# Self-attention over eight images on one core: row maxima brought to their row by small copies instead of TensorE turns

## The chip, the core and the metric

The kernel runs on one core of a Trainium2 chip. A core has TensorE (PE in the profile; its weight loads are shown apart as PEld), VectorE (DVE), ScalarE (ACT), GpSimd (POOL) and SyncE (SP), each with its own instruction stream; they meet only at semaphores. Here SP only issues copies (DMAs), which 16 DMA engines carry out. The metric is the device time of one execution in microseconds; of several executions the median is taken. The profile describes one execution.

## What is computed

For each of 8 images with 128 channels and 32x32 = 1024 pixels, a 1x1-convolution attention block:

```python
xf = x.reshape(b, c, n)                       # n = 1024
q = einsum('oc,bcn->bon', Wq, xf) + bq        # 64 channels
k = einsum('oc,bcn->bon', Wk, xf) + bk        # 64 channels
v = einsum('oc,bcn->bon', Wv, xf) + bv        # 128 channels
attn = softmax(einsum('bci,bcj->bij', q, k), axis=-1)
out = einsum('bcn,bmn->bcm', v, attn)
return gamma * out + x
```

All of it is float32. The kernel splits operands into a rounded high part (fp32r) and a rest, so that fast matmuls keep the accuracy.

## The kernel before, in words

**Steps.** The work is cut into 8 images x 2 halves x 8 tiles = 128 steps. Step s belongs to image b = s // 16 and to place k = s % 16 in it. A half (512 query pixels) is called a chunk; chunk c = 2b + h has the steps 8c to 8c + 7. At step s TensorE does, in this order: the scores of step s + 2 (`score_tile`, two matmuls of 512 columns, L510 and L511), one or two matmuls for row maxima of a later chunk (`do_max`, L468), the weighted sums of step s - 2 (`sums_hi`, four matmuls of 258 columns, L529; after every fourth step also `sums_lo`, 16 matmuls, L545), and then the side jobs of that place in the image: the projections `qk` (L455 to L457) and `v` (L462) of a coming image, the turning of a finished output chunk `out` (L478), and `mt`.

**The row maxima.** The softmax needs the maximum of each query's scores before its exponentials. For a chunk, eight matmuls (L468, two for each of its four query tiles) give scores in PSUM; DVE reduces each to `neg_max` (L740), and `round_max` (L747) makes of them `neg_max_r`, 128 partitions x 4 columns: queries lie across the partitions. The scores matmul L511 wants them along one row instead, `q_lomax[64, chunk]`, which the row of ones in `k_hione` adds to every score. Before the change the job `mt` does this: four turns on TensorE against `identity_r` (L473, `turn_max`) into a PSUM bank, and an ACT copy of one row of 512 (L660, `write_max_rows`), which raises `max_rows_done`. `mt` stands at the end of step k = 4 (for the second chunk of the same image) and of k = 12 (for the first chunk of the next).

**Two banks.** `work` has two PSUM banks. The jobs mx (a maximum's matmul), qk, v, mt and out take them in turn, in the order `WORK_ORDER`; each waits until the job two places ahead of it has been read out. After a `qk` job, for instance, the second job behind it waits until ACT has written `qk_hi` (L643) and DVE `qk_lo` (L731) from that bank.

**Copies between partitions.** `spread(n)` on SP sends q and k of image n to the partitions where the matmuls want them: six copies of 256 KB, four of which (semaphore `spread_mx`) the first maximum matmul of image n waits for, and two (`spread_rest`) its first scores. It waits until image n - 2 has no scores left to do, since the buffers alternate; `spread(b + 2)` thus starts at place k = 13 of image b. `store_y` stores an output chunk, `load_x` loads an image. SP does all of these in a fixed order.

**Exponentials.** ACT makes two exponentials a step from a scores bank (L676 and L679); the scores of step s + 2 wait for the second of step s, since there are two scores banks.

## Time and profile before

| | us |
|---|---|
| median of 3 runs | 248.56 (247.63 to 250.33) |
| the profiled execution, its own time | 247.75 |
| the profiled execution, its span | 246.0 |
| PE busy | 233.6 (95%) |
| ACT busy | 189.0 (77%) |
| POOL busy | 176.5 (72%) |
| DVE busy | 170.7 (69%) |

The span runs from the first to the last instruction; 1.75 us of the execution's time lie around it. A matmul's busy time is its own stretch from start to modelled end, and matmuls overlap, so for TensorE the distance from one start to the next says what an instruction costs; the starts in the rows below are read for that. TensorE's clock stood at full speed over the whole span (0.997 on average).

### The profile page before, as it was taken

The page shows a single profiled execution, that of the slowest core. Times are in us where ns is not written, and L with a number is a line of the kernel's source. Part 1 is how long each engine was busy: PE and PEld are TensorE (multiplying, and loading weights), DVE is VectorE, ACT ScalarE, POOL GpSimd, SP SyncE. Part 2 cuts the span into 40 slices and gives each one's busy share as a digit, 9 for nine tenths or more (in the row PEclk, how much of TensorE's full clock was granted, in tenths as well). Part 3 has the DMA queues.
Part 4 walks back from the last instruction along what each step waited for, and adds up shares of the span by engine and source line. Part 5 has one row for each costly group of instructions (what it writes and reads, how often), then busy time and mean ns, then how long its engine had stood idle before and what let it go on. Part 6 is the DMA issues. An engine that isn't in the chain of part 4 may idle for free.

```text
span 246.0 us, 4933 instructions
## 1 busy us (share of the span) xinstructions
PE 233.6 (95%) x1738; PEld 200.3 (81%) x1738; DVE 170.7 (69%) x287; ACT 189.0 (77%) x359; POOL 176.5 (72%) x158
## 2 busy tenths in 40 slices
PE   7998988999999999999999999999999999999992
PEld 7365867888879898898879888898888889898891
DVE  1667295876888767776878767877768767784354
ACT  2868956788787888779877887788877878879841
POOL 8578986299963897469962898558982877668760
PEclk9999999999999999999999999999999999999998
DMA  4706400570409312390407504191105601010102
GB/s 97 237 29 145 113 0 4 128 173 3 128 0 223 79 45 87 85 217 0 131 0 174 129 0 129 34 229 40 45 0 124 177 3 45 0 45 0 44 15 73
DMA packets 8040, 19.85 MB, mean 81 GB/s; under 512 B 1744, under 2 KB 2256, under 8 KB 8016
## 3 DMA queue, kind: packets, MB, share of 16 engines
q1 hardware_dynamic: 7776, 19.50, 30.3%
q8 instruction: 14, 0.23, 0.4%
q14 instruction: 10, 0.08, 0.1%
q10 hardware_dynamic: 240, 0.03, 0.1%
HBM read 4.33 MB, written 4.19 MB: 35 GB/s over the span
## 4 chain that ended last, share of the span: by engine, by line
PE 88%; ACT 5%; DVE 5%; issue 1%; POOL 0%; POOLq 0%; DVEq 0%; ACTq 0%
PE sums L529 24%; PE sums L545 12%; PE scores L510 12%; PE work L468 11%; PE scores L511 11%; PE work L462 5%; PE work L478 3%; DVE qk_lo L731 2%; ACT qk_hi L643 2%; PE work L473 2%; PE sums L559 2%; PE work L457 1%; PE work L456 1%; PE work L455 1%; DVE neg_max L740 1%
## 5 line engine op out<-in xcount | busy, mean ns | idle before, releaser
L392 POOL TENSOR_TENSOR weight_lo<-weight,weight_hi 128x512 bf16<-128x512 f32 x90 | 124.5, 1402 | 48.6 <-ACT weight_hi L679 48.2
L740 DVE TENSOR_REDUCE neg_max<-work 128x1 f32<-128x512 f32 x120 | 81.7, 686 | 25.5 <-PE work L468 25.3
L676 ACT ACTIVATE weight<-scores 128x512 f32<-128x512 f32 x128 | 76.6, 599 | 22.6 <-PE scores L511 18.9
L529 PEld LDWEIGHTS sums<-values,weight_hi 128*128 128x128 f32 x512 | 78.1, 188 | 9.9 <-issue 0.5
L529 PE MATMUL sums<-values,weight_hi 128*128 128x258 f32 x512 | 81.7, 282 | 0.1
L679 ACT ACTIVATE weight_hi<-scores 128x512 fp32r<-128x512 f32 x128 | 76.5, 597 | 0.0
L510 PE MATMUL scores<-q_hihi,k_hilo 128*128 128x512 f32 x128 | 55.1, 430 | 1.2 <-ACT weight_hi L679 1.1
L511 PE MATMUL scores<-q_lomax,k_hione 128*128 128x512 f32 x128 | 50.4, 394 | 0.0
L468 PE MATMUL work<-k_hilo,q_hihi 128*128 128x512 f32 x120 | 48.6, 411 | 1.7 <-DVE qk_lo L731 0.9
L779 DVE TENSOR_TENSOR weight_lo<-weight,weight_hi 128x512 bf16<-128x512 f32 x38 | 35.7, 940 | 2.4 <-ACT weight_hi L679 2.4
L545 PE MATMUL sums<-values_b,weight_lo 128*128 128x130 bf16 x512 | 35.5, 221 | 0.0
L468 PEld LDWEIGHTS work<-k_hilo,q_hihi 128*128 128x128 f32 x120 | 22.5, 187 | 13.7 <-DVE values L736 3.8
L545 PEld LDWEIGHTS sums<-values_b,weight_lo 128*128 128x128 bf16 x512 | 29.8, 98 | 1.6
L510 PEld LDWEIGHTS scores<-q_hihi,k_hilo 128*128 128x128 f32 x128 | 24.2, 189 | 2.9 <-ACT weight_hi L679 1.9
L511 PEld LDWEIGHTS scores<-q_lomax,k_hione 128*128 128x128 f32 x128 | 24.3, 190 | 0.6
L787 DVE TENSOR_TENSOR total<-sums,low_sum 128x258 f32<-128x258 f32 x32 | 13.6, 427 | 13.9 <-ACT low_sum L685 13.3
L685 ACT ACTIVATE low_sum<-sums 128x256 f32<-128x256 f32 x32 | 12.4, 387 | 7.2 <-PE sums L545 5.1
L399 POOL TENSOR_TENSOR scaled<-total,one_over 128x512 f32<-128x512 f32 x15 | 15.6, 1042 | 0.0
L462 PE MATMUL work<-w_v_t,x_sb 128*128 128x128 f32 x112 | 15.5, 281 | 0.0
L373 POOL TENSOR_TENSOR x_lo<-x_sb,x_hi 128x512 fp32r<-128x512 f32 x12 | 15.5, 1288 | 0.0
L384 POOL TENSOR_SCALAR values_b<-values 128x512 bf16<-128x512 f32 x16 | 9.9, 620 | 7.6 <-ACT values L654 7.6
L736 DVE TENSOR_TENSOR values<-work,values 128x512 fp32r<-128x512 f32 x14 | 9.7, 692 | 7.3 <-ACT values L654 7.3
(78 smaller groups left out, 186.4 us busy)
## 6 DMA issues: line engine op xcount, KB each, us to landing
out<-y_sb SPq DMA_DIRECT2D x15, 256.0 KB, 2.5
x_sb<-in_x SPq DMA_DIRECT2D x7, 512.0 KB, 4.4
q_hihi<-qk_hi SPq DMA_DIRECT2D x14, 256.0 KB, 4.4
k_hilo<-qk_hi SPq DMA_DIRECT2D x7, 256.0 KB, 3.1
k_hilo<-qk_lo SPq DMA_DIRECT2D x7, 256.0 KB, 5.1
q_lomax<-qk_lo SPq DMA_DIRECT2D x7, 256.0 KB, 5.2
k_hione<-qk_hi SPq DMA_DIRECT2D x7, 256.0 KB, 5.1
x_sb<-in_x SPq DMA_DIRECT2D x2, 256.0 KB, 3.5
```

The source lines that it names most:

```text
L392: pool.tensor_tensor(weight_lo[:, r], weight[:, r], weight_hi[:, r], ALU.subtract).then_inc(weight_lo_pool_done, 1)
L399: pool.tensor_tensor(scaled[:, :], total[:, :, 0:CHANNELS], by, ALU.mult).then_inc(scaled_done, 1)
L462: last = pe.matmul(place[:, tile(t)], image(n)[:, tile(half * CHUNK_TILES + t)], w_v_t[:, :], start=True, stop=True)
L468: pe.matmul(place, q_hihi[p][:, tile(t)], k_hilo[p][:, chunk(h)], start=True, stop=True).then_inc(mx_done, 1)
L510: pe.matmul(scores[:, s % 2], k_hilo[p][:, tile(j)], q_hihi[p][:, chunk(h)], start=True, stop=False)
L511: pe.matmul(scores[:, s % 2], k_hione[p][:, tile(j)], q_lomax[p][:, chunk(h)], start=False, stop=True).then_inc(scores_done, 1)
L529: last = pe.matmul(sums[:, it, 0:VCOLS], weight_hi[:, r, tile(it)], values[p][:, j], start=(j == 0), stop=False)
L545: return pe.matmul(sums[:, it, CHANNELS:VCOLS], weight_lo[:, i % RING, tile(it)], values_b[p][:, j], start=False, stop=(j == TILES - 1))
L676: act.activation(weight[:, r], scores[:, s % 2], ACT.Exp)
L679: act.activation(weight_hi[:, r], scores[:, s % 2], ACT.Exp).then_inc(weight_hi_done, 1)
L740: dve.reduce_max(neg_max[:, h, t:t + 1], place, AX.X, negate=True).then_inc(neg_max_done, 1)
L779: dve.tensor_tensor(weight_lo[:, r], weight[:, r], weight_hi[:, r], ALU.subtract).then_inc(weight_lo_done, 1)
```

## The change

The job `mt` is gone except for chunks 0 and 1. For the chunks 2 to 15 SP sends the maxima itself: `send_max_row` issues four copies, each of one column of `neg_max_r` (128 partitions x 4 bytes) into 128 elements of the row of `q_lomax`. The scores of such a chunk wait for `max_row_sent` and no longer for `max_rows_done`. The maxima of a chunk are found two steps earlier (chunk c in steps 8c - 14 to 8c - 7, before 8c - 12 to 8c - 5). Two maxima of chunk 1 move ahead of the first step, the place of six idle turns (`keep_busy`) there is taken by the second projection of image 1, whose `qk_lo` moves on DVE behind the maxima of step 0. The maxima of image 1 (chunks 2 and 3) follow a table over steps 5 to 17. `neg_max` is laid out with its two halves side by side, and `round_max` is a reduction over them.

```diff
-WARM_UP = (14, 4, 6)
+WARM_UP = (14, 4)
...
+EARLY = 18
+EARLY_MAXES = {5: (2, 0, 1), 6: (2, 1, 2), 7: (2, 3, 1), 8: (2, 4, 2), 9: (2, 6, 1), 10: (2, 7, 1),
...
 def max_jobs(s):
-    if s < 4:
-        return [(1, 2 * s), (1, 2 * s + 1)]
-    if s < 12:
-        return [(2, 2 * (s - 7)), (2, 2 * (s - 7) + 1)] if 7 <= s < 11 else []
-    chunk = (s + 12) // TILES
-    return [(chunk, (s + 12) % TILES)] if chunk < CHUNKS else []
+    if s < 3:
+        return [(1, 2 * s + 2), (1, 2 * s + 3)]
+    if s < EARLY:
+        c, first, count = EARLY_MAXES.get(s, (0, 0, 0))
+        return [(c, i) for i in range(first, first + count)]
+    chunk = (s + 14) // TILES
+    return [(chunk, (s + 14) % TILES)] if chunk < CHUNKS else []
...
-    if k == 4:
-        jobs.append(("mt", 2 * b + 1, 0))
+    if b == 0 and k == 4:
+        jobs.append(("mt", 1, 0))
...
-    if k == 12 and b + 1 < BATCHES:
-        jobs.append(("mt", 2 * b + 2, 0))
...
+FIRST_MAXES = [("mx", 1, 0), ("mx", 1, 1)]
+WORK_ORDER = FIRST_MAXES + [job for s in range(ALL_STEPS)
+                            for job in [("mx", c, i) for c, i in max_jobs(s)] + side_jobs(s)]
...
+        def wait_max_row(engine, c):
+            if c < HALVES:
+                engine.wait_ge(max_rows_done, c + 1)
+            else:
+                engine.wait_ge(max_row_sent[c % 2], 16 * CHUNK_TILES * (c // 2))
...
+            def send_max_row(c):
+                n, h = divmod(c, HALVES)
+                sp.wait_ge(neg_max_r_done, c + 1)
+
+                wait(sp, scores_done, STEPS * (n - 2) + TILES * (h + 1))
+                for t in range(CHUNK_TILES):
+                    at = h * CHUNK_TILES + t
+                    row = q_lomax[n % 2][HEAD:HEAD + 1, tile(at)].bitcast(fp32)
+                    sp.dma_start(row.rearrange("a (i b) -> a i b", b=1),
+                                 neg_max_r[:, at:at + 1].bitcast(fp32)).then_inc(max_row_sent[c % 2], 16)
...
             for b in range(BATCHES):
                 if b > 0:
+                    send_max_row(2 * b + 1)
                     store_y(2 * b - 1)
                     if b + IMAGES - 1 < BATCHES:
                         load_x(b + IMAGES - 1)
+                if b + 1 < BATCHES:
+                    send_max_row(2 * b + 2)
                 if b + 2 < BATCHES:
                     spread(b + 2)
                 store_y(2 * b)
...
                 if j == 0:
-                    pe.wait_ge(max_rows_done, HALVES * b + h + 1)
+                    wait_max_row(pe, HALVES * b + h)
...
-            for h in range(HALVES):
-                pe.wait_ge(neg_max_done, CHUNK_TILES + h + 1)
-                project_qk(1, h, sums[:, h])
+            pe.wait_ge(first_hi_done, len(FIRST))
+            for name, c, i in FIRST_MAXES:
+                do_max(c, i)
+            pe.wait_ge(neg_max_done, CHUNK_TILES + 1)
+            project_qk(1, 0, sums[:, 0])
             pe.wait_ge(neg_max_r_done, 1)
             pe.wait_ge(pool_setup, SETUP_MADE)
             turn_max(0, sums[:, 2])
-            keep_busy(WARM_UP[2], sums[:, 3])
+            project_qk(1, 1, sums[:, 1])
...
-                wait(dve, mt_done, c - 1)
-                dve.tensor_tensor(neg_max_r[:, cols], neg_max[:, 0, cols], neg_max[:, 1, cols],
-                                  ALU.min).then_inc(neg_max_r_done, 1)
+                if c < 2 * HALVES:
+                    wait(dve, mt_done, c - 1)
+                else:
+                    wait_max_row(dve, c - HALVES)
+                dve.tensor_reduce(neg_max_r[:, cols], neg_max[:, cols], AX.X, ALU.min).then_inc(neg_max_r_done, 1)
...
-            for h in range(HALVES):
-                rest_of_qk(1, h, sums[:, h])
+            for name, c, i in FIRST_MAXES:
+                do_max(c, i)
+            rest_of_qk(1, 0, sums[:, 0])
...
+                if s == 0:
+                    rest_of_qk(1, 1, sums[:, 1])
```

The order on TensorE before, from the second `qk` job (k = 11) of an image in the middle to the maximum of k = 13; lines are those of the kernel before:

```order
L455 MATMUL work<-x_hi,w_qk_hi 128x512
L456 MATMUL work<-x_hi,w_qk_lo 128x512
L457 MATMUL work<-x_lo,w_qk_hi 128x512
L510 MATMUL scores<-q_hihi1,k_hilo1 128x512
L511 MATMUL scores<-q_lomax1,k_hione1 128x512
L468 MATMUL work<-k_hilo0,q_hihi0 128x512
L529 MATMUL sums<-values1,weight_hi 128x258 x4
L473 MATMUL work<-identity_r,neg_max_r 1x128 x4
L510 MATMUL scores<-q_hihi1,k_hilo1 128x512
L511 MATMUL scores<-q_lomax1,k_hione1 128x512
L468 MATMUL work<-k_hilo0,q_hihi0 128x512
```

The same piece of the changed kernel, with its own line numbers (the `qk` job is L482 to L484, scores L537 and L538, a maximum L495, sums L556):

```order
L482 MATMUL work<-x_hi,w_qk_hi 128x512
L483 MATMUL work<-x_hi,w_qk_lo 128x512
L484 MATMUL work<-x_lo,w_qk_hi 128x512
L537 MATMUL scores<-q_hihi1,k_hilo1 128x512
L538 MATMUL scores<-q_lomax1,k_hione1 128x512
L495 MATMUL work<-k_hilo0,q_hihi0 128x512
L556 MATMUL sums<-values1,weight_hi 128x258 x4
L537 MATMUL scores<-q_hihi1,k_hilo1 128x512
L538 MATMUL scores<-q_lomax1,k_hione1 128x512
L495 MATMUL work<-k_hilo0,q_hihi0 128x512
```

The four turns are gone; the job that stands second behind `qk`, and so waits for its `qk_lo`, is now the last row, a maximum's matmul one pair of scores later.

The order on SP before, over one image, from one `spread` to the next:

```order
L302 DMA k_hilo<-qk_lo 64x1024 [waits qk_lo_done]
L303 DMA q_lomax<-qk_lo 64x1024
L304 DMA k_hione<-qk_hi 64x1024
L308 DMA out<-y_sb 128x512 [waits y_done] x2
L291 DMA x_sb<-in_x 128x1024
L298 DMA k_hilo<-qk_hi 64x1024 [waits scores_done,qk_hi_done]
```

And in the changed kernel (L327 is a copy of one column of maxima, L332 a store, L304 the load of an image, L311 the first copy of the next `spread`):

```order
L315 DMA k_hilo<-qk_lo 64x1024 [waits qk_lo_done]
L316 DMA q_lomax<-qk_lo 64x1024
L317 DMA k_hione<-qk_hi 64x1024
L332 DMA out<-y_sb 128x512 [waits y_done]
L327 DMA q_lomax<-neg_max_r 1x128x1 [waits scores_done,neg_max_r_done]
L327 DMA q_lomax<-neg_max_r 1x128x1 x3
L332 DMA out<-y_sb 128x512 [waits y_done]
L304 DMA x_sb<-in_x 128x1024
L327 DMA q_lomax<-neg_max_r 1x128x1 [waits scores_done,neg_max_r_done]
L327 DMA q_lomax<-neg_max_r 1x128x1 x3
L311 DMA k_hilo<-qk_hi 64x1024 [waits scores_done,qk_hi_done]
```

Two groups of four small copies stand between the large ones: one between the two stores, one ahead of the next `spread`.

## Rows read from the trace of the kernel before

**Rows 1.** The page, part 1: busy time and share of the span

```profile
PE 233.6 (95%) x1738; PEld 200.3 (81%) x1738; DVE 170.7 (69%) x287; ACT 189.0 (77%) x359; POOL 176.5 (72%) x158
```

**Rows 2.** Waits: who waited for whom; us in total, times, longest

```profile
PE work L473 <- DVE qk_lo L731: 2.4, 6, 0.4
...
PE scores L510 <- ACT weight_hi L679: 1.1, 2, 0.7
```

**Rows 3.** Timeline of PE, image 2, k = 12 and 13: start, us, instruction

```profile
99.26 0.64 PE L529 MATMUL sums<-values,weight_hi 128*128 128x258 f32 x4
100.28 0.40 PE L473 MATMUL work<-identity_r,neg_max_r 128*1 128x128 f32 x4 [0.39 <-DVE qk_lo L731]
100.52 0.44 PE L510 MATMUL scores<-q_hihi,k_hilo 128*128 128x512 f32 x1
100.80 0.40 PE L511 MATMUL scores<-q_lomax,k_hione 128*128 128x512 f32 x1
```

**Rows 4.** Timeline of PE, image 3, k = 2 to 5

```profile
110.51 0.64 PE L529 MATMUL sums<-values,weight_hi 128*128 128x258 f32 x4
110.99 0.40 PE L510 MATMUL scores<-q_hihi,k_hilo 128*128 128x512 f32 x1
111.22 0.40 PE L511 MATMUL scores<-q_lomax,k_hione 128*128 128x512 f32 x1
...
112.92 0.64 PE L529 MATMUL sums<-values,weight_hi 128*128 128x258 f32 x4
113.39 0.40 PE L473 MATMUL work<-identity_r,neg_max_r 128*1 128x128 f32 x4
113.63 0.44 PE L510 MATMUL scores<-q_hihi,k_hilo 128*128 128x512 f32 x1
113.91 0.40 PE L511 MATMUL scores<-q_lomax,k_hione 128*128 128x512 f32 x1
```

**Rows 5.** Busy time by stretch, one image from spread to spread

```profile
core 0: us, PE busy (x) PEld busy (x) DVE busy (x) ACT busy (x) POOL busy (x), PEclk, DMA share, GB/s
101.28:129.62 28.34, 27.94 (x216) 24.43 (x214) 21.43 (x36) 23.13 (x45) 21.04 (x18) 1.00 0.36 94
```

**Rows 6.** Timeline of DVE: qk_lo of k = 11, last maximum of k = 1

```profile
99.48 0.75 DVE L731 SCALAR_TENSOR_TENSOR qk_lo<-work,b_qk,qk_hi 128x512 fp32r<-128x512 f32 x1 [0.84 <-ACT qk_hi L643]
...
107.64 0.69 DVE L740 TENSOR_REDUCE neg_max<-work 128x1 f32<-128x512 f32 x1 [0.23 <-PE work L468]
```

**Rows 7.** Timeline of PE, early steps: waits at k = 8, 10 and 12 of image 0

```profile
33.80 0.50 PE L468 MATMUL work<-k_hilo,q_hihi 128*128 128x512 f32 x1 [0.87 <-DVE qk_lo L731]
...
39.49 0.50 PE L468 MATMUL work<-k_hilo,q_hihi 128*128 128x512 f32 x1 [0.71 <-DVE values L736]
...
43.68 0.40 PE L473 MATMUL work<-identity_r,neg_max_r 128*1 128x128 f32 x4 [0.40 <-DVE qk_lo L731]
```

**Rows 8.** Timeline of SP: start and length of the issue of each copy

```profile
4.67 0.43 SPq L317 DMA_DIRECT2D b_v<-in_L_conv_bv  x1
...
21.58 1.15 SPq L302 DMA_DIRECT2D k_hilo<-qk_lo  x1
...
101.28 0.47 SPq L298 DMA_DIRECT2D k_hilo<-qk_hi  x1
...
103.10 1.14 SPq L302 DMA_DIRECT2D k_hilo<-qk_lo  x1
```

**Rows 9.** Timeline of PE: maximum of k = 2, scores at k = 6, image 3

```profile
110.28 0.39 PE L468 MATMUL work<-k_hilo,q_hihi 128*128 128x512 f32 x1
...
115.81 0.48 PE L510 MATMUL scores<-q_hihi,k_hilo 128*128 128x512 f32 x1
```

**Rows 10.** DMA view of 100 to 112 us: engines busy by 0.3 us, us to landing

```profile
DMA  0000000099995999998999989999999987200000
...
k_hilo<-qk_lo SPq DMA_DIRECT2D x1, 256.0 KB, 4.9
...
out<-y_sb SPq DMA_DIRECT2D x1, 256.0 KB, 4.8
```

**Rows 11.** The page, part 6: a copy of 128 elements of 4 bytes

```profile
b_v<-in_L_conv_bv SPq DMA_DIRECT2D x1, 0.5 KB, 2.6
```

More of the change, by code:

```diff
@@ L42 @@
 SPREAD_MX, SPREAD_REST = 4, 2
+EARLY = 18
+EARLY_MAXES = {5: (2, 0, 1), 6: (2, 1, 2), 7: (2, 3, 1), 8: (2, 4, 2), 9: (2, 6, 1), 10: (2, 7, 1),
+               11: (3, 0, 1), 12: (3, 1, 2), 13: (3, 3, 1), 14: (3, 4, 1), 15: (3, 5, 1), 16: (3, 6, 1), 17: (3, 7, 1)}
 def max_jobs(s):
-    if s < 4:
-        return [(1, 2 * s), (1, 2 * s + 1)]
-    if s < 12:
-        return [(2, 2 * (s - 7)), (2, 2 * (s - 7) + 1)] if 7 <= s < 11 else []
-    chunk = (s + 12) // TILES
-    return [(chunk, (s + 12) % TILES)] if chunk < CHUNKS else []
+    if s < 3:
[5 more added lines that the diff above has]
+    return [(chunk, (s + 14) % TILES)] if chunk < CHUNKS else []
 def side_jobs(s):
@@ L73, in side_jobs @@
     return jobs
-WORK_ORDER = [job for s in range(ALL_STEPS)
-              for job in [("mx", c, i) for c, i in max_jobs(s)] + side_jobs(s)]
+FIRST_MAXES = [("mx", 1, 0), ("mx", 1, 1)]
+WORK_ORDER = FIRST_MAXES + [job for s in range(ALL_STEPS)
+                            for job in [("mx", c, i) for c, i in max_jobs(s)] + side_jobs(s)]
 PLACE = {job: n for n, job in enumerate(WORK_ORDER)}
@@ L168, in attention_program @@
         values_b = [sbuf(f"values_b{p}", [TILE, TILES, CHANNELS + 2], bf16) for p in range(2)]
-        neg_max = sbuf("neg_max", [TILE, 2, TILES], fp32)
+        neg_max = sbuf("neg_max", [TILE, TILES, 2], fp32)
         neg_max_r = sbuf("neg_max_r", [TILE, TILES], fp32r)
@@ L227, in attention_program @@
         max_rows_done = sem("max_rows_done")
+        max_row_sent = [sem(f"max_row_sent{p}") for p in range(2)]
         w_ready = sem("w_ready")
@@ L597, in _ @@
             turn_max(0, sums[:, 2])
-            keep_busy(WARM_UP[2], sums[:, 3])
+            project_qk(1, 1, sums[:, 1])
             pe.wait_ge(first_q_lo_done, HALVES)
-            pe.wait_ge(first_hi_done, len(FIRST))
             for s in range(AHEAD):
@@ L739, in maximum @@
             def maximum(t, h, place):
-                dve.reduce_max(neg_max[:, h, t:t + 1], place, AX.X, negate=True).then_inc(neg_max_done, 1)
+                dve.reduce_max(neg_max[:, t, h:h + 1], place, AX.X, negate=True).then_inc(neg_max_done, 1)
             def round_max(c):
```

## The prediction

> **What bounds the kernel now.** I began with the busy times [rows 1]: PE has 95% of the span, ACT 77%, POOL 72%, DVE 69%. A busy PE says little, as its matmuls overlap, so I read PE's timeline by starts. Between spread and spread lies one image, 28.34 us [rows 5]; in it nothing but PE comes near (ACT 23.1, DVE 21.4, POOL 21.0). The reader should see there that matmuls follow each other at fixed distances: a 512-column matmul 0.23 us after the one before, a group of four sums 0.48 us [rows 4], with hardly any waiting. The table of waits confirms it: after the first microseconds TensorE waits for little but banks, and the largest single item that belongs to the part that changes is the turn of the maxima behind `qk_lo`, 2.4 us in 6 waits [rows 2]. So PE's instruction stream is the path, and what leaves it counts in full, as long as nothing new is late.
>
> **A set of turns.** At k = 4 the set starts at 113.39 and the scores behind it at 113.63, 0.24 us; the second scores matmul then comes after 0.28 instead of 0.23; the sums ahead take 0.47 instead of 0.48 [rows 4]. One set costs 0.28 to 0.29 us. Fifteen sets run within the steps and 14 go. The Trainium skill, page "TensorE: Matmul & The Clock Gate", section on PE-mode transpose, gives about 275 ns for one 128x128 transpose in a kernel's context; by that figure a set would be 1.1 us and 14 sets 15.4 us, an estimate. The starts here contradict it: four turns in 0.24 us.
>
> **The wait ahead of k = 12's set.** From the sums at 99.26 to the turns at 100.28 are 1.02 us, where 0.48 would do: 0.54 us waiting for the bank of `qk`, which DVE's `qk_lo` of 99.48 to 100.23 gives back [rows 3, 6]. With the set gone, the second job behind `qk` is the maximum of k = 13. It comes after two scores matmuls: 99.26 + 0.48 + 2 x 0.23 = 100.20, against 100.28 when the bank is free. A matmul that had to wait also delays its successor by about 0.1 (its busy time reads 0.50 instead of 0.40 [rows 7, 9]). So some 0.18 of the 0.54 stays and 0.36 goes. Images 1 to 5 have this: 5 x 0.36 = 1.8 us. From below, the same wait could come back in full at the new place (0); from above it could all go (2.7).
>
> **The early steps (image 0).** Gone: a set (0.29); the wait for `values` at k = 10, since one maximum and not two stands behind `v` there (0.71 + about 0.2 of its train) [rows 7]; a short wait ahead of the first `qk`, about 0.3. Added: two maxima more before step 18 (0.46). The second maximum of k = 12 now waits for `qk_lo` ahead of the sums, so that this wait grows by about the 0.5 that the sums used to cover. The `qk_lo` of image 1 moves behind two maxima on DVE, by about 0.9 us, and SP's fourth copy of `spread(1)`, at 21.58 before, waits for it [rows 8]: with 4.9 us to landing [rows 10] it lands near 27.3, while the first maximum of chunk 2 now stands at step 5, near 26.9. That is a wait of about 0.5 us, and DVE's longer chain over steps 0 to 2 adds 0.4. Of these two, some 0.5 is taken up by the wait of 0.87 us at k = 8 [rows 7]. Gains 1.5, costs 1.9, absorbed 0.5: about +0.2 us net, and I would believe anything from -1 to +1.2. In the prologue, two maxima and one projection take the place of two projections, and the other projection that of the idle turns: about equal.
>
> **The end.** The two maxima that were moved early leave the last image: 2 x 0.23 = 0.46 us off. ACT has room there for one step more without a maximum.
>
> **The new wait.** It must be asked what is queued behind each new thing. On SP, the group for the second chunk of an image stands behind `store_y(2b)`, that for the first chunk of the next image behind `store_y` and `load_x`, both ahead of their deadlines. The tight one is the second chunk: its last maximum is now that of k = 1, reduced by 108.33, rounded by about 108.5 [rows 6]. No row shows such a copy between partitions. The nearest is b_v, also 128 elements of 4 bytes: issued in 0.43 us, landed after 2.6 [rows 8, 11]. Four of these: the last is issued near 109.9. The DMA engines are still full with `spread` and the store until about 110.5 [rows 10], so I let it land at 112.6 to 113.1. The scores of k = 6 that need it start at 115.81, or 115.5 without the set of k = 4 [rows 9]. That leaves over 2 us, and I cost the copies at nothing; their cover is these four steps of TensorE's own work. The far bound is the 256 KB copy of `qk_lo`, 1.15 us an issue and 4.9 to landing [rows 8, 10]: 108.5 + 3 x 1.15 + 4.9 = 116.9, 1.4 us too late. The first chunks have about 4 us to spare.
>
> The maxima also need their `spread` two steps earlier, at k = 2 instead of 4. The fourth copy is issued at 103.10 and lands 4.9 us later, at 108.0; the maximum of k = 2 stands at 110.28 [rows 8 to 10]. Two microseconds remain, or 1.1 if the 4.9 counts from the end of the issue. The small copies ahead of `spread` on SP go out some 5 us before it starts.
>
> DVE's reduction instead of a minimum of 128x4, and ACT's 14 row copies less, lie beside the path: nothing.
>
> **The sum.** 13 sets outside image 0 x 0.29 = 3.8; wait 1.8; image 0 +0.2; end 0.46. Together 6.2 us. Against the profiled execution's own 247.75 us this is 241.5; the median of the runs shown is 0.8 above that execution and gives 242.4. I say 242.0. By the bounds above the gain is 3.2 (early steps at -1, the wait returning) to 8.1 (early +1.2, the wait all gone), so this case spans 239.7 to 245.3, and I expect it mostly within 240.5 to 243.5.
>
> **Rivals.**
> *The copies are late (slower).* If four copies with 4-byte elements behave like the large ones, the scores of k = 6 wait 1.4 us in each of the six images 1 to 6 (image 7 has no `spread` ahead of it), and the first chunks, due near 130.1 and landing near 122.5 + 3 x 1.15 + 4.9 = 130.9, 0.8 us in each of seven: 8.4 + 5.6 = 14 us lost against 6.2 gained, 247.75 + 7.8 = 255.6. It decides from 116.5 us on, that is from 8 us between the rounded maximum and the last landing, where I expect 4.5. For it: each element is one small write to a single partition, and the DMA engines are full when the copies are issued. Against it: the b_v row. Chance 0.07. Two sections of the Trainium skill's page "DMA: Bandwidth & Descriptors" bear on it and point in opposite directions. Specifications: under 512 B a write is a read-modify-write, which speaks against the change. On the semaphore's 16: a copy is spread over up to 16 engines by the size of the slowest dimension of both sides, here 128 and 128, so each engine gets 8 elements and not one engine all 128. No row of this case shows either.
>
> *PE runs into the others' latencies.* Jobs closer together meet banks that are not yet free: the waits for `qk_lo` and `values` of 0.87 and 0.71 us [rows 7] in image 0 show what tight spacing costs. Half a microsecond in each of six images takes 3 us back: 245 (244.5 to 245.5). Against it: in the middle images such waits are under 0.1 us, and at most one job's order changes. The same price holds where rows land half a microsecond late. Chance 0.15.
>
> *Nothing changes.* The early steps lose 1 us, the wait returns in full at k = 13, and the copies are late by half a microsecond in every image: 6.2 - 1.2 - 1.8 - 3 = 0.2, about 248. For the path to stay where it is three small things must coincide. Chance 0.06.
>
> *More than the sum.* If turns cost TensorE more than their starts show, for instance by stalls that I cannot separate, 239.5. Chance 0.07. By the skill's 275 ns it would be near 232; I give that under 0.01, as the starts exclude it.
>
> The forecast keeps 0.65. Within 1% (2.5 us of 248.56, about what a measurement of this kernel can tell from no change) means 246.1 to 251.0. Faster holds the forecast, the larger gain and nearly all of the 245 case: 0.86. Same holds the last rival and a little of the 245 case: 0.07. Slower: 0.07. The range of 8 in 10 runs from 240.2 to 246.0; it leaves out the slower case, no change and part of the larger gain.
>
> **What would show it.** In the profile after: 8 turns of maxima and not 64; an image of 27.4 us instead of 28.34, spread to spread; a wait of TensorE for `qk_lo` at the maximum of k = 13 of under 0.2 us; no wait of the scores for a copy; small copies on SP of about 0.45 us each, landing in under 3.5 us; near step 5 a wait of TensorE of about 0.5 us behind the fourth copy of `spread(1)`. I am wrong if TensorE is idle at k = 6 or k = 2 of the middle images behind a DMA, or if the period stays above 28 us.

## The result

| | before | after |
|---|---|---|
| median of 4 runs each, us | 248.09 (247.48 to 250.33) | 241.16 (240.90 to 241.74) |
| ratio, 95% interval | | 0.9708 (0.9642 to 0.9773) |
| profiled execution / its span, us | 247.75 / 246.0 | 241.74 / 239.7 |
| PE, ACT, POOL, DVE busy, us | 233.6, 189.0, 176.5, 170.7 | 229.3, 179.6, 174.6, 169.5 |

The change makes the kernel 3% faster. The same kernel run again later, as the partner of the experiments, took 240.44 us (240.29 to 241.56, 6 runs) against 248.64, ratio 0.9681 (0.9651 to 0.9712). The forecast was 242.0, with a range of 240.2 to 246.0.

The page of the changed kernel, parts 1 and 6, answers to [rows 1]:

```profile
PE 229.3 (96%) x1676; PEld 196.8 (82%) x1676; DVE 169.5 (71%) x287; ACT 179.6 (75%) x345; POOL 174.6 (73%) x158
...
q_lomax<-neg_max_r SPq DMA_DIRECT2D x56, 0.5 KB, 2.1
```

PE is still the path. The last row is new: 56 small copies (14 chunks of four), landing a median 2.1 us after their issue.

One image from spread to spread, the view of [rows 5]:

```profile
98.91:126.23 27.32, 27.32 (x207) 23.95 (x208) 21.42 (x36) 21.81 (x43) 20.78 (x17) 1.00 0.40 98
```

An image takes 27.32 us instead of 28.34. The clock is at its full level in both, and ACT has two row copies less.

TensorE in image 2, k = 12 and 13, the place of [rows 3] (timeline: start, us, instruction):

```profile
97.72 0.64 PE L556 MATMUL sums<-values,weight_hi 128*128 128x258 f32 x4
98.20 0.39 PE L537 MATMUL scores<-q_hihi,k_hilo 128*128 128x512 f32 x1
98.43 0.40 PE L538 MATMUL scores<-q_lomax,k_hione 128*128 128x512 f32 x1
98.76 0.50 PE L495 MATMUL work<-k_hilo,q_hihi 128*128 128x512 f32 x1
99.11 0.64 PE L556 MATMUL sums<-values,weight_hi 128*128 128x258 f32 x4
```

Where 1.02 us lay between the sums and the turns, the scores now start 0.48 after the sums. What is left of the wait for the bank of `qk` stands ahead of the maximum of k = 13: it starts 0.33 after L538 instead of 0.23, and the sums 0.35 after it instead of 0.24 (0.24 as in the rows of k = 2 below, 108.10 to 108.33), together 0.2 us.

TensorE in image 3, the maximum of k = 2 and the scores of k = 6, the places of [rows 9]:

```profile
107.86 0.40 PE L538 MATMUL scores<-q_lomax,k_hione 128*128 128x512 f32 x1
108.10 0.39 PE L495 MATMUL work<-k_hilo,q_hihi 128*128 128x512 f32 x1
108.33 0.64 PE L556 MATMUL sums<-values,weight_hi 128*128 128x258 f32 x4
...
112.35 1.11 PE L572 MATMUL sums<-values_b,weight_lo 128*128 128x130 bf16 x16
113.27 0.48 PE L537 MATMUL scores<-q_hihi,k_hilo 128*128 128x512 f32 x1
```

Neither has a wait in brackets. The two stations of SP and DVE behind them are these (SP: issue; DVE: last maximum of k = 1 and its rounding):

```profile
100.76 1.17 SPq L315 DMA_DIRECT2D k_hilo<-qk_lo  x1
...
106.37 2.44 SPq L327 DMA_DIRECT2D q_lomax<-neg_max_r  x4
```

```profile
105.46 0.69 DVE L768 TENSOR_REDUCE neg_max<-work 128x1 f32<-128x512 f32 x1 [0.23 <-PE work L495]
106.18 0.16 DVE L778 TENSOR_REDUCE neg_max_r<-neg_max 128x4 fp32r<-128x8 f32 x1
```

The maxima are rounded at 106.34, the four copies are issued from 106.37 to 108.81, and the scores that need them start at 113.27, 4.5 us behind the end of the last issue. In the DMA view of 98.9 to 112 us the engines (one digit for 0.33 us) are full up to about 107.8 and at two tenths or less from 108.1 on, so the copies get through behind the store without trouble:

```profile
DMA  0007999599989999978999998994222020000000
```

**Where the 6.3 us of span went.** I cut both traces at the same instructions: the first scores (17.31 before, 17.79 after) and the first copy of `spread` (L298 before, L311 after) of images 2 and 7 (44.69 and 186.20 before, 44.54 and 180.84 after).

| stretch | before | after | gain |
|---|---|---|---|
| start to first scores | 17.31 | 17.79 | -0.48 |
| to `spread(2)` | 27.38 | 26.75 | 0.63 |
| five images, to `spread(7)` | 141.51 | 136.30 | 5.21 |
| to the end of the span | 59.8 | 58.9 | 0.9 |

The loss in the first stretch is not the change's. The first projection of that execution takes 1.88 us for two matmuls, where before the change it takes 1.02:

```profile
5.64 1.88 PE L598 MATMUL scores<-x_sb,w_kk_t 128*128 128x512 f32 x2
```

Its input was not late, for it starts at 5.64 as it did before (5.63); its matmuls are slow. They lie 0.86 us apart (5.64, 6.50, 7.35) where they lay 0.43 apart (5.63, 6.06, 6.49). The granted clock reads 1.00 in both, so the cause stays open. The profiles of experiments 8 and 9 show the same, others a part of it.

In the profile of the changed kernel's second set of runs it takes 1.02, the first scores start at 16.79, and the four stretches gain 0.52, 0.65, 5.13 and 1.2, together 7.5 (span 238.5). From the first projection to the first scores are 11.68 us before and 11.27 there, so the rewritten prologue is worth 0.4.

### The profile page after: what moved, and what is told of

Same layout as the page of the kernel before. It is cut to its first block, busy times and chain, and to the rows that moved or that the text cites. A ratio compares the mean times of both kernels' runs of the same rounds, so it can differ in the third digit from the quotient of the medians.

```text
span 239.7 us, 4848 instructions
## 1 busy us (share of the span) xinstructions
PE 229.3 (96%) x1676; PEld 196.8 (82%) x1676; DVE 169.5 (71%) x287; ACT 179.6 (75%) x345; POOL 174.6 (73%) x158
## 4 chain that ended last, share of the span: by engine, by line
PE 92%; DVE 3%; ACT 3%; issue 1%; POOL 0%; POOLq 0%; DVEq 0%
PE sums L556 25%; PE sums L572 13%; PE scores L537 12%; PE work L495 12%; PE scores L538 12%; PE work L489 6%; PE work L505 3%; PE sums L586 2%; PE work L483 1%; PE work L484 1%; PE work L482 1%; DVE neg_max L768 1%; DVE qk_lo L759 1%; PE scores L489 1%; PE sums L478 1%
## 5 line engine op out<-in xcount | busy, mean ns | idle before, releaser
L419 POOL TENSOR_TENSOR weight_lo<-weight,weight_hi 128x512 bf16<-128x512 f32 x90 | 122.5, 1381 | 43.6 <-ACT weight_hi L707 43.4
L556 PEld LDWEIGHTS sums<-values,weight_hi 128*128 128x128 f32 x512 | 78.1, 188 | 10.2 <-issue 0.5
L556 PE MATMUL sums<-values,weight_hi 128*128 128x258 f32 x512 | 81.7, 282 | 0.1
L537 PE MATMUL scores<-q_hihi,k_hilo 128*128 128x512 f32 x128 | 54.5, 426 | 1.1 <-ACT weight_hi L707 1.1
L495 PE MATMUL work<-k_hilo,q_hihi 128*128 128x512 f32 x120 | 48.9, 413 | 2.4 <-DVE qk_lo L759 2.0
L538 PE MATMUL scores<-q_lomax,k_hione 128*128 128x512 f32 x128 | 50.4, 393 | 0.0
L809 DVE TENSOR_TENSOR weight_lo<-weight,weight_hi 128x512 bf16<-128x512 f32 x38 | 36.5, 961 | 2.7 <-ACT weight_hi L707 2.7
L495 PEld LDWEIGHTS work<-k_hilo,q_hihi 128*128 128x128 f32 x120 | 22.4, 188 | 14.5 <-DVE qk_lo L759 6.5
L537 PEld LDWEIGHTS scores<-q_hihi,k_hilo 128*128 128x128 f32 x128 | 24.2, 189 | 3.2 <-ACT weight_hi L707 1.9
L538 PEld LDWEIGHTS scores<-q_lomax,k_hione 128*128 128x128 f32 x128 | 24.3, 190 | 0.6
```

Of the source, the lines that this page charges most:

```text
L419: pool.tensor_tensor(weight_lo[:, r], weight[:, r], weight_hi[:, r], ALU.subtract).then_inc(weight_lo_pool_done, 1)
L495: pe.matmul(place, q_hihi[p][:, tile(t)], k_hilo[p][:, chunk(h)], start=True, stop=True).then_inc(mx_done, 1)
L537: pe.matmul(scores[:, s % 2], k_hilo[p][:, tile(j)], q_hihi[p][:, chunk(h)], start=True, stop=False)
L538: pe.matmul(scores[:, s % 2], k_hione[p][:, tile(j)], q_lomax[p][:, chunk(h)], start=False, stop=True).then_inc(scores_done, 1)
L556: last = pe.matmul(sums[:, it, 0:VCOLS], weight_hi[:, r, tile(it)], values[p][:, j], start=(j == 0), stop=False)
L809: dve.tensor_tensor(weight_lo[:, r], weight[:, r], weight_hi[:, r], ALU.subtract).then_inc(weight_lo_done, 1)
```

## The experiments

All are the changed kernel with one edit; the kernel before ran beside them (median 248.61 to 248.65). A difference of two of these kernels is taken against 240.44, the changed kernel's second result. The reading to be tested: the turns' time on TensorE comes back in full, and the copies cost nothing as long as they land in time. Against it stood: the gain is due to ACT's missing copies or to the new order of the maxima; the copies cost something by themselves; and they land so close to the need that little would make them late.

**1. The turns alone put back** (`e1_turns_back`), same maxima, same copies: turns of columns of `identity_r` into the bank, at the old places and in the old order of banks, with nothing done with the result.

```diff
-    if b == 0 and k == 4:
+    if k == 4:
...
+    if k == 12 and b + 1 < BATCHES:
+        jobs.append(("mt", 2 * b + 2, 0))
...
+                elif name == "mt":
+                    for t in range(CHUNK_TILES):
+                        pe.transpose(place[0:1, tile(t)].bitcast(fp32r), identity_r[:, t:t + 1], identity_r[:, :])
```

> The changed kernel with the turns alone put back: at k = 4 and k = 12 TensorE again does four turns into a bank (of columns of the identity, their result is read by nobody; the maxima still travel by copies), and the jobs stand in the bank order of before. No ACT row copies. Theory A (TensorE's instruction stream is the path, and what left it is the gain): 14 sets at 0.35 us, the difference of k = 4 and 5 between the two traces, give 4.9 us, and the wait for qk_lo comes back ahead of the set of k = 12 in five images, about 0.33 each, 1.7: 241.2 + 6.6 = 247.8, between 247 and 248.5. Rival B (ACT's 14 row copies, or the chain from maxima to scores, were the cost): stays within 1 us of 241.2.

Measured: 246.70 us (245.78 to 247.55, 7 runs), ratio 0.9917 (0.9883 to 0.9951): a little below the band. An image takes 28.26 us again, and the wait is back at its old place:

```profile
99.75 0.64 PE L561 MATMUL sums<-values,weight_hi 128*128 128x258 f32 x4
100.79 0.40 PE L529 MATMUL work<-identity_r 128*1 128x128 f32 x4 [0.40 <-DVE qk_lo L764]
101.03 0.44 PE L542 MATMUL scores<-q_hihi,k_hilo 128*128 128x512 f32 x1
```

By the medians, 6.3 of the 8.2 us of the change come back with the turns and the wait in front of them. The middle of the two traces shows it most cleanly: the five images from `spread(2)` to `spread(7)` take 141.20 us here (45.34 to 186.54), 141.51 before the change and 136.38 in the changed kernel's second profile, so 4.8 of 5.1 us are back, 0.96 an image. Outside these images it isn't a pure price of the turns: in image 0 the extra set at k = 12 also shifts which bank the maxima there get, and one of them, at 34.81, waits 2.35 us for `qk_lo` where the changed kernel waits 1.16. By the medians it stays 1.9 us below the kernel before; of what it keeps of the change, prologue, order of the maxima and end, no run shows the shares. The two profiled executions are only 0.2 us apart (247.55 and 247.75), so the size of this rest is uncertain too.

**2. ACT's 14 copies put back** (`e2_act_copies_back`), into a spare row, in the old places.

```diff
...
+                if (k == 4 and b > 0) or (k == 12 and b + 1 < BATCHES):
+                    act.activation(spare_row[HEAD:HEAD + 1, :], k_hione[0][HEAD:HEAD + 1, chunk(0)], ACT.Copy)
```

> The changed kernel with 14 ACT copies of one row of 512 put back at the places of before (k = 4 and k = 12), between two places in SBUF that nobody else uses; no turns. Theory A: ACT has idle time at both places, no change, 240.8 to 241.8. Rival B (ACT's 0.59 us a copy was on the path): up to 14 x 0.59 = 8.2 us more, 249.

Measured: 240.95 us (240.24 to 241.07, 4 runs), ratio 0.9685 (0.9648 to 0.9722). ACT is busy 189.8 us instead of 179.6, and the time doesn't move. ACT's work left out was off the path.

**3. The maxima as late as before** (`e3_maxima_late`): copies, but the old schedule.

```diff
...
-    chunk = (s + 14) // TILES
-    return [(chunk, (s + 14) % TILES)] if chunk < CHUNKS else []
+    chunk = (s + 12) // TILES
+    return [(chunk, (s + 12) % TILES)] if chunk < CHUNKS else []
...
-FIRST_MAXES = [("mx", 1, 0), ("mx", 1, 1)]
+FIRST_MAXES = []
```

> The changed kernel with the maxima where they were before (chunk c in steps 8c - 12 to 8c - 5, the first steps by the old list, no maxima ahead of step 0), rows still sent by copies. By the trace of the changed kernel: the last maximum of a second chunk (k = 3) would be rounded near 110.6 instead of 106.3, the fourth copy issued 1.85 us later lands 2.2 to 2.3 us after that, at 114.7, and the scores of k = 6 want it at 113.3: 1.4 us late, seven times; first chunks land near 128.3 against 127.8, 0.5 late, seven times. Theory A with a copy's latency of about 4.1 us from the rounded maxima to the last landing: 241.2 + 9.8 + 3.5 + 0.5 for the first steps = 255, between 251 and 257. Rival (the copies are quick enough, and moving the maxima was not needed): 241 to 242.5.

Measured: 256.65 us (254.52 to 258.35, 4 runs), ratio 1.0293 (1.0218 to 1.0369), inside the band. The table of waits names the cause (us in total, times, longest):

```profile
PEld scores L536 <- DMA q_lomax<-neg_max_r: 14.2, 13, 2.1
...
PE scores L536 <- DMA q_lomax<-neg_max_r: 11.4, 10, 2.0
```

In image 3 the copies are issued from 113.99 (SP) and the scores start at 117.90 (PE), so from the first issue to usable scores are 3.9 us:

```profile
116.61 0.22 PE L571 MATMUL sums<-values_b,weight_lo 128*128 128x130 bf16 x1
117.90 0.50 PE L536 MATMUL scores<-q_hihi,k_hilo 128*128 128x512 f32 x1 [1.07 <-DMA q_lomax<-neg_max_r]
```

Copies in place of the turns are worth something only together with the earlier maxima: alone they cost 8.0 us against the kernel before.

**4. One step late instead of two** (`e4_maxima_one_step_late`): from step 18 on `s + 13` for `s + 14`, and the table without its last entry.

```diff
-               11: (3, 0, 1), 12: (3, 1, 2), 13: (3, 3, 1), 14: (3, 4, 1), 15: (3, 5, 1), 16: (3, 6, 1), 17: (3, 7, 1)}
+               11: (3, 0, 1), 12: (3, 1, 2), 13: (3, 3, 1), 14: (3, 4, 1), 15: (3, 5, 1), 16: (3, 6, 1)}
...
-    chunk = (s + 14) // TILES
-    return [(chunk, (s + 14) % TILES)] if chunk < CHUNKS else []
+    chunk = (s + 13) // TILES
+    return [(chunk, (s + 13) % TILES)] if chunk < CHUNKS else []
```

> The changed kernel with the maxima of chunks 4 to 15 one step later (8c - 13 to 8c - 6; the last maximum of chunk 3 at step 18). Theory A: the maximum of k = 2 is reduced behind the values job, rounded near 109.9, the last copy lands near 114.0 against 113.3 wanted: 0.7 to 0.8 us late in seven images; first chunks just in time: 241.2 + 5.3 = 246.5, between 244.5 and 247.5. Rival: no change, 241 to 242, if a step of slack is to spare.

Measured: 247.91 us (247.17 to 248.17, 10 runs), ratio 0.9952 (0.9925 to 0.9979), above what I gave it.

```profile
PEld scores L537 <- DMA q_lomax<-neg_max_r: 7.0, 9, 1.5
```

```profile
114.79 0.51 PE L537 MATMUL scores<-q_hihi,k_hilo 128*128 128x512 f32 x1 [1.09 <-DMA q_lomax<-neg_max_r]
```

In image 3 the copies start at 110.15 and, this time, take 3.18 us to issue instead of 2.44; the scores wait 1.09 us and start at 114.79, 4.6 us later. In image 2 the issue takes 2.44 us (from 82.19 on), and the scores start 3.9 us later (86.10) with a wait of 0.35. The expectation had 4.1 us to the landing in every image. It missed two more things: the first chunk of image 7, expected just in time, waits 1.28 us behind an issue of 3.29 (208.56), and a wait costs more than its bracket says: from scores to scores against the changed kernel's second profile, the nine places lose 7.1 us together, with 5.4 us in brackets (TensorE's own row of the waits). One step of slack is thus not enough; the change lives on the second one.

**5. Twice the copies** (`e5_eight_copies`): four more to a spare row, ahead of the four that count.

```diff
...
+                    row = spare_rows[c % 2][HEAD:HEAD + 1, tile(t)]
+                    sp.dma_start(row.rearrange("a (i b) -> a i b", b=1),
+                                 neg_max_r[:, at:at + 1].bitcast(fp32)).then_inc(max_row_sent[c % 2], 16)
```

> The changed kernel with eight small copies a chunk: four of the same columns into a row that nobody reads are issued ahead of the real four. By the trace of the changed kernel the copies of a second chunk are issued from 106.4 us on, 2.45 us for four, and the last of four lands near 110.5; with four more ahead of it, near 113.0, and the scores want it at 113.3. Theory A (the copies are hidden, and cost nothing while they land in time): no change, 240.7 to 241.9. Rival C (each copy costs a little wherever it lies, by loading the DMA engines or SBUF): as much again as the first four cost, seen as a longer image than 27.3 us.

Measured: 244.48 us (244.39 to 246.38, 6 runs), ratio 0.9864 (0.9828 to 0.9901). I had expected no change, and that failed. The loss is not spread over the images, though. It stands where the first scores of a chunk wait for their copies: compared start by start with the changed kernel's second profile, the first scores of five chunks lose 2.2, 0.5, 0.4, 0.3 and 0.1 us, 3.5 of the 4.0 us between the two profiled executions. The largest is at chunk 2, whose copies go out in image 0 (SP, then PE):

```profile
39.55 2.44 SPq L328 DMA_DIRECT2D spare_rows<-neg_max_r  x4
42.04 3.64 SPq L333 DMA_DIRECT2D q_lomax<-neg_max_r  x4
```

```profile
47.13 0.50 PE L543 MATMUL scores<-q_hihi,k_hilo 128*128 128x512 f32 x1 [2.01 <-DMA q_lomax<-neg_max_r]
...
115.10 0.50 PE L543 MATMUL scores<-q_hihi,k_hilo 128*128 128x512 f32 x1 [0.32 <-DMA q_lomax<-neg_max_r]
```

Chunk 2's last maximum stands only at step 10. In the changed kernel its copies are issued from 40.53 on, and the scores start at 45.90 without a wait, 2.9 us behind the last issue; four issues more ahead of them use that up. An image in which nothing waits takes 27.3 us as before (72.92 to 100.23), with 2048 small elements sent in it instead of 1024. The copies cost by lateness and not by load.

**6. The old prologue** (`e6_prologue_before`): first maxima and both projections as before the change.

```diff
-WARM_UP = (14, 4)
+WARM_UP = (14, 4, 6)
...
-    if s < 3:
-        return [(1, 2 * s + 2), (1, 2 * s + 3)]
+    if s < 4:
+        return [(1, 2 * s), (1, 2 * s + 1)]
...
-FIRST_MAXES = [("mx", 1, 0), ("mx", 1, 1)]
+FIRST_MAXES = []
```

> The changed kernel with the prologue alone undone: both projections of image 1 and the six idle turns as before, no maxima ahead of step 0, chunk 1's maxima two a step in steps 0 to 3. The trace of the changed kernel reaches the first scores some 0.4 us sooner after the values projection than the one of before, and DVE's chain over steps 0 to 2 is the same length: 241.2 + 0.4 to + 1.0 = 241.6 to 242.2. Rival (the prologue is not on the path, or costs as much as it gives): 241.2 within 0.3.

Measured: 241.49 us (240.68 to 243.50, 6 runs), ratio 0.9740 (0.9696 to 0.9784). The interval overlaps with that of the changed kernel (0.9651 to 0.9712), and the median is 1.05 us above 240.44, so the time alone doesn't decide. The traces point the same way: from the first projection to the first scores 5.38 to 17.16 here, 11.78 us, against 11.27; 0.1 of it are slower first matmuls (7.20 - 5.38 = 1.82 us to the third projection, 1.72 there), which leaves 0.4.

**7. Another table for images 0 and 1** (`e7_other_table`), so that a single maximum stands behind `qk` and waits less at 34.30 us, where the changed kernel waits 1.16.

```diff
-EARLY_MAXES = {5: (2, 0, 1), 6: (2, 1, 2), 7: (2, 3, 1), 8: (2, 4, 2), 9: (2, 6, 1), 10: (2, 7, 1),
-               11: (3, 0, 1), 12: (3, 1, 2), 13: (3, 3, 1), 14: (3, 4, 1), 15: (3, 5, 1), 16: (3, 6, 1), 17: (3, 7, 1)}
+EARLY_MAXES = {5: (2, 0, 2), 6: (2, 2, 2), 7: (2, 4, 1), 8: (2, 5, 1), 9: (2, 6, 1), 10: (2, 7, 1),
+               11: (3, 0, 1), 12: (3, 1, 1), 13: (3, 2, 2), 14: (3, 4, 1), 15: (3, 5, 1), 16: (3, 6, 1), 17: (3, 7, 1)}
```

> The changed kernel with another list for the maxima of image 1: two at steps 5, 6 and 13, one at steps 7 to 12 and 14 to 17, so that no second maximum stands right behind a qk job. In the trace of the changed kernel the second maxima of steps 8 and 12 wait 1.16 and 0.89 us for qk_lo. Theory A (TensorE's waits there are on the path): most of both goes, 241.2 - 1.5 = 239.7, between 239.2 and 240.4. Rival (another engine takes over in the first steps, DVE or ACT): within 0.5 of 241.2.

Measured: 240.17 us (239.84 to 240.83, 5 runs), ratio 0.9675 (0.9643 to 0.9707). The number lies in the band of theory A, but only because the expectation stood on 241.2; against 240.44 it is 0.3 us less, no different from the changed kernel, so theory A isn't borne out by it. The two waits for `qk_lo` went, and most of it came back at another place: the second maximum at step 5 needs the bank of the last turn set, which ACT still reads.

```profile
26.96 0.40 PE L495 MATMUL work<-k_hilo,q_hihi 128*128 128x512 f32 x1
28.24 0.50 PE L495 MATMUL work<-k_hilo,q_hihi 128*128 128x512 f32 x1 [0.88 <-ACT q_lomax L688]
```

**8. The later image's projections one step later** (`e8_qk_one_step_later`), at k = 8 and 12, so that the maximum of the next step comes after DVE has read out `qk`'s bank. Its table has two maxima at steps 5, 6 and 11.

```diff
...
-    if k in (7, 11) and b + 2 < BATCHES:
-        jobs.append(("qk", b + 2, (7, 11).index(k)))
+    if k in (8, 12) and b + 2 < BATCHES:
+        jobs.append(("qk", b + 2, (8, 12).index(k)))
```

> As the other table (two maxima at steps 5, 6 and 11), and the qk jobs of all images at k = 8 and 12 instead of 7 and 11, so that the 16 matmuls of sums_lo lie between a qk job and the maximum that waits for its bank. In the changed kernel the maxima of k = 9 and 13 each lose about 0.2 us that way. Theory A: 0.4 less in each of six images, 2.4, and 1.5 in the first steps: 241.2 - 3.9 = 237.3, between 236.8 and 239. Rival D: the spread of the image after next starts later, by the qk_lo that it waits for, and the maximum of k = 2 waits for it: within 1 us of 241.2, with TensorE idle at k = 2.

Measured: 237.76 us (237.26 to 238.32, 6 runs), ratio 0.9574 (0.9542 to 0.9605), inside the band. `qk_lo` is gone from the list of what TensorE's maxima wait for (in the changed kernel 2.0 us on PE and 6.5 on its weight loads), and an image takes 26.96 us. The wait of 0.88 at step 5 is still there.

**9. The same with step 5 back at one maximum** (`e10_first_list`).

```diff
-EARLY_MAXES = {5: (2, 0, 1), 6: (2, 1, 2), 7: (2, 3, 1), 8: (2, 4, 2), 9: (2, 6, 1), 10: (2, 7, 1),
-               11: (3, 0, 1), 12: (3, 1, 2), 13: (3, 3, 1), 14: (3, 4, 1), 15: (3, 5, 1), 16: (3, 6, 1), 17: (3, 7, 1)}
+EARLY_MAXES = {5: (2, 0, 1), 6: (2, 1, 2), 7: (2, 3, 2), 8: (2, 5, 1), 9: (2, 6, 1), 10: (2, 7, 1),
+               11: (3, 0, 2), 12: (3, 2, 1), 13: (3, 3, 1), 14: (3, 4, 1), 15: (3, 5, 1), 16: (3, 6, 1), 17: (3, 7, 1)}
...
-    if k in (7, 11) and b + 2 < BATCHES:
-        jobs.append(("qk", b + 2, (7, 11).index(k)))
+    if k in (8, 12) and b + 2 < BATCHES:
+        jobs.append(("qk", b + 2, (8, 12).index(k)))
```

> As the kernel with the qk jobs at k = 8 and 12, with the second maximum of step 5 moved to step 7: there TensorE waited 0.88 us for the bank of chunk 1's turned maxima. Theory A: that wait goes, and the copies of chunk 2 are no later: 237.8 - 0.8 = 237.0, between 236.6 and 237.5. Rival: the first steps are held by ACT or DVE, no change, 237.8.

Measured: 236.51 us (236.24 to 237.39, 6 runs), ratio 0.9518 (0.9490 to 0.9545), just below the band and the fastest of all, 3.9 us below the changed kernel. Against experiment 8 that is 1.25 us by the medians and 0.8, as forecast, by the spans of the two profiled executions (235.6 and 236.4). One image (windows):

```profile
96.69:123.61 26.92, 26.92 (x208) 24.04 (x207) 20.44 (x35) 21.86 (x43) 21.10 (x18) 1.00 0.41 99
```

**10. The change again** (`e9_change_again`), unedited, beside 9 and 11.

> The changed kernel itself once more, beside the other runs of this call, for a closer ratio: 241.2, a ratio of 0.971 within 0.004.

Measured: 240.44 us, as given above; an image takes 27.33.

**11. A set of turns by itself** (`e11_turns_at_4`): only at k = 4 of the images 1 to 7, seven sets, where no wait stands in front of them.

```diff
-    if b == 0 and k == 4:
-        jobs.append(("mt", 1, 0))
+    if k == 4:
+        jobs.append(("mt", 2 * b + 1, 0))
```

> The changed kernel with turns put back only at k = 4 of images 1 to 7 (columns of the identity, result unread, no wait for maxima), seven sets, where no bank wait came with them before. Theory A: a set costs 0.35 us, by the difference of k = 4 and 5 between the traces: 241.2 + 2.45 = 243.6, between 243.2 and 244.2. By the 0.29 us that the prediction took from the starts alone: 243.2. Rival E (a set costs far more or less than its starts show, for instance 1.1 us, or nothing as it hides beside other work): 248.9, or 241.2.

Measured: 242.23 us (242.11 to 242.57, 5 runs), ratio 0.9743 (0.9716 to 0.9771). That is below the band. Of the 1.4 us to the forecast 243.6, 0.8 are the changed kernel's own (240.44 for 241.2) and 0.7 the price of the sets: against 240.44 there are 1.79 us for seven, 0.26 each and not 0.35. Five images take 137.75 (43.83 to 181.58) against 136.38 (43.52 to 179.90 in the changed kernel's second profile), 0.27 each. The rows agree:

```profile
111.06 0.41 PE L527 MATMUL work<-identity_r 128*1 128x128 f32 x4
111.30 0.44 PE L540 MATMUL scores<-q_hihi,k_hilo 128*128 128x512 f32 x1
111.58 0.40 PE L541 MATMUL scores<-q_lomax,k_hione 128*128 128x512 f32 x1
```

Again 0.24 to the scores, and 0.28 from scores to scores.

## Why the prediction was right, and where its sizes were off

The forecast case came true, by its own mechanism: TensorE's instruction stream is the path, what leaves it counts, and nothing new is late. Against the profiled execution's own 247.75 us the sum gave 6.2 us; the two profiled executions of the changed kernel lie 6.0 and 7.3 below it. Of the signs named in advance, these came: 8 turns of maxima, an image of 27.3 us, about 0.2 us of wait at the maximum of k = 13, no scores that wait for a copy, a landing under 3.5 us (at most 3.0). Two did not: a small copy takes SP 0.60 us and not 0.45, and there is no wait near step 5.

**The set of turns** (0.28 to 0.29 us): confirmed by experiment 11 with 0.26 to 0.27 in time and 0.24 plus 0.04 in the starts. The estimate by the Trainium skill, "TensorE: Matmul & The Clock Gate", section on PE-mode transpose, of about 275 ns for one turn and so 1.1 us a set, did not hold: four small turns together cost about what it gives for one. The row shows why. A single turn's own busy time is 0.22 us, near the page's figure, but four of them start 0.06 us apart (from 113.39 on), so a time for one turn must not be multiplied by their number.

**The wait ahead of k = 12's set** (0.54, of which 0.18 would stay): about 0.2 stayed. With two sets the images should be 0.94 shorter; they are 5.21 / 5 = 1.04 in one profile and 5.13 / 5 = 1.03 in the other. Where the 0.1 over it lies I can name by the starts, not by an experiment. From the scores of one step to those of the next, image 3 (starts of L510 and L537) gains 0.26 at k = 4 (1.42 to 1.16) and 0.80 at k = 12 (1.97 to 1.17), loses 0.14 at k = 13, as forecast, and gains 0.09 at k = 5 (2.18 to 2.09). That 0.09 is not the turns' either: by experiment 11 a set costs 0.27 in all, k = 5 included.

**Image 0** (+0.2, between -1 and +1.2): it gained 0.63 and 0.65, inside the bounds but 0.4 off. Three things in that working were wrong. It charged 0.46 for two maxima more within the steps; but the two that moved early stand in the prologue, and the steps up to 17 hold 22 maxima before and after. That was counted twice. And the 0.5 us wait near step 5 behind the fourth copy of `spread(1)` did not come: that copy is issued at 22.65, and the maximum starts at 27.31, right behind the scores of 27.08, so the copy had landed after at most 4.7 us instead of the 4.9 that I took from the middle of the kernel. And the 0.4 us for DVE's longer chain over steps 0 to 2 does not show: from the first scores to the turns of step 4 are 9.16 us before and 8.77 after, 0.39 less. On the other side the first wait behind `qk_lo` came out longer, 1.16 us at 34.30 against 0.87 in [rows 7], where the working had 0.5 of it taken up; the second, 0.89 at 43.00 against 0.40, is the 0.5 that was forecast. The terms as written also add up to about +0.1 and not +0.2. That the total came so near is thus partly luck: errors of both signs.

**The prologue** ("about equal"): 0.4 us gained, by both profiles of the changed kernel and the comparison with experiment 6. In place of six idle turns and a wait for ACT's row there is a projection.

**The end** (0.46, and three sets): 1.3 forecast, 0.9 and 1.2 found.

**The new wait** (copies at nothing): right for the time, and the slack that I named for the second chunks, "over 2 us", is about right: in image 3 experiment 4 issues the copies 3.8 us later (110.15 for 106.37), for scores that would be due 0.4 later (113.7 for 113.27), and they wait 1.09: that leaves 2.3, with an issue 0.7 us longer than usual, and about 3 with the usual one. The chain from rounded maxima to the last landing was put at 4.5 us; from there to the waiting scores experiments 3 and 4 measure 3.9 to 4.7. The issue was taken too short, 0.43 us by the b_v row [rows 8]; it is 0.60, four in 2.44, in some groups up to 3.6. The landing was taken longer, 2.6 against 2.1, and the two errors nearly cancel. I called the first chunks comfortable ("about 4 us to spare") and overlooked chunk 2, the first chunk of image 1, whose maxima end only at step 10; experiment 5 showed that it has less slack than four more issues take.

**The rivals.** Late copies (255.6): not here, but it is the mechanism of experiments 3 and 4, and 3's 256.65 us shows its size. The Trainium skill's page "DMA: Bandwidth & Descriptors" was cited for both directions (Specifications, and the section on the semaphore's 16); copies of 4-byte elements land in 2.1 us, less than the large ones, so whatever the read-modify-write costs is small here. PE running into the others' latencies: in image 0 the two waits behind `qk_lo` grew by 0.8 us together while that at k = 10 (0.71) went; in the middle images nothing of the kind came. Experiments 8 and 9 show what it still costs: 0.4 us an image for the bank of `qk`. Nothing changes: excluded. More than the sum: the second set of runs comes near it, 7.3 against 6.2, but by prologue, image 0 and 0.1 us an image, and not by dearer turns, as experiment 11 shows.

What stays open: how a single copy for all four columns would do in place of four, which wasn't tried; which part of the 1.9 us that experiment 1 keeps is due to which edit; and why the first matmuls of some executions run at half their pace.

## What to carry to other kernels

When the engine that bounds a kernel does a small rearrangement, look for a route that it doesn't take part in, and then ask not what the route costs but how many microseconds earlier its input must be ready; here four copies need about 4 us, now and then 4.7, two steps, and without these the same change loses 3%. A wait for a buffer ahead of the instruction that goes away is part of its price, and what is left of it sits at the next user of the buffer, where moving the producer by one step may remove it (experiments 8 and 9). Where a schedule is shifted, count its items in each stretch on both sides, so that none is charged twice.

## What the runs showed of the hardware

**TensorE's clock fell after one wait of 2 us, and not after another.** In experiment 3 the scores at 134.60 waited 1.95 us for their copies. Until then the granted clock was 1.00; from 134 to 139 us it was 0.66 on average, and from 136 to 139 it was 0.50, the lower of the two levels (1.2 GHz); then it was 1.00 again (windows; the number behind the bracketed counts is the clock):

```profile
130.00:134.00 4.00, 2.65 (x26) 2.01 (x24) 3.37 (x4) 1.91 (x4) 1.34 (x2) 1.00 0.38 67
134.00:139.00 5.00, 4.40 (x18) 3.98 (x19) 2.58 (x4) 2.06 (x4) 0.00 (x0) 0.66 0.92 214
139.00:144.00 5.00, 5.00 (x44) 4.57 (x43) 3.16 (x7) 3.56 (x9) 4.19 (x3) 1.00 0.44 107
```

The starts show it too: 0.43 us from a 512-column matmul to the next, and 0.23 again from 139.05 on.

```profile
137.36 0.63 PE L537 MATMUL scores<-q_lomax,k_hione 128*128 128x512 f32 x1
137.79 0.63 PE L494 MATMUL work<-k_hilo,q_hihi 128*128 128x512 f32 x1
138.22 1.00 PE L555 MATMUL sums<-values,weight_hi 128*128 128x258 f32 x4
139.05 0.39 PE L536 MATMUL scores<-q_hihi,k_hilo 128*128 128x512 f32 x1
139.28 0.39 PE L537 MATMUL scores<-q_lomax,k_hione 128*128 128x512 f32 x1
```

From the scores at 134.60 to those at 139.05 are 4.45 us; the same work in image 2, at full clock, takes 2.89 (103.84 to 106.73). The fall thus cost 1.6 us. Not every wait of this length has it: in experiment 5 the scores at 47.13 waited 2.01 us, the granted clock stayed at 1.00 and the same work took 2.90 (47.13 to 50.03); nor had the other nine waits in experiment 3, 0.16 to 1.52 us long. What decides it, no run here shows. It does not explain the 16.2 us that experiment 3 lost against the change either: it happens once in the profiled execution, and another one with a mean clock of 1.000 still took 254.52 us, 14.1 above 240.44. Most of it is the 14.2 us that the weight loads waited for the copies.

**The first matmuls can run at half their pace.** In the profile of the changed kernel the first two projection matmuls lie 0.86 us apart, before the change 0.43, with the granted clock read as 1.00 in both.

**Issue of small copies.** A copy of one column (128 elements of 4 bytes, partition to row) keeps SP 0.60 us and lands after a median of 2.1 us (1.9 at least, 3.5 at most over the runs); the four of image 3, issued while the DMA engines are still full, have a median of 2.3. A single issue took up to 1.70 us. Doubling these copies changed no image in which nothing waited for them.
